# A fused conditioning and mixture-of-experts kernel: first silu and a gate product moved up, eight comparisons on GpSimd, one weight load and three second matrices moved in SyncE's queue

## The reference

```python
w = weights[conditions]                      # [32, 32, 32], itok picks the rows
xt = einsum('bct,bcd->bdt', x, w)            # x is 32 x 32 x 256: T = 1024 tokens, D = 256
probs = softmax(xt @ w_router)               # 16 experts
top_w, top_i = top_k(probs, 4); top_w /= sum(top_w)
g = silu(xt @ we1[e]) * (xt @ we3[e])        # H = 128, for each chosen expert
moe = sum over the chosen of top_w * (g @ we2[e])
shared = silu(xt @ ws1) * (xt @ ws3) @ ws2   # HS = 512, four units of 128
out = x + shared / 5 + moe * 4 / 5
```

## Time and profile before

| | |
|---|---|
| median of three runs | 146.99 us (146.42 to 147.77) |
| profiled execution | 146.96 us, span 145.2 us |
| TensorE busy | 132.4 us, 91% of the span |
| VectorE, ScalarE, GpSimd busy | 102.8, 71.6 and 65.6 us |
| granted TensorE clock | 1.0 of full speed |
| DMA | 29.82 MB, mean 205 GB/s |

### The profile page before, as it was taken

One profiled execution on the slowest core, in us unless ns is written; L12 is line 12 of the kernel. 1 busy time (PEld: TensorE's weight loads), 2 busy tenths in 40 slices (PEclk: granted clock), 3 DMA queues, 4 the chain that ended last, 5 costly groups with the idle time before them and its releaser, 6 DMA issues.

```text
span 145.2 us, 2783 instructions
## 1 busy us (share of the span) xinstructions
PE 132.4 (91%) x800; PEld 111.2 (77%) x800; DVE 102.8 (71%) x271; ACT 71.6 (49%) x164; POOL 65.6 (45%) x79
## 2 busy tenths in 40 slices
PE   5997998599989599999999999999999999999680
PEld 2437677388758488999999999999999978888560
DVE  1301799997769977877898989876677653157992
ACT  4003797999547454346353645377434331008900
POOL 0600000002777877656666776767576777100000
PEclk9999999999999999999999999999999999999999
DMA  1823799988955667687677755544542222399924
GB/s 36 294 59 84 218 287 272 379 247 257 365 204 167 188 188 207 163 251 227 184 249 232 254 212 220 187 165 169 186 178 86 97 108 103 74 387 423 385 79 144
DMA packets 23742, 29.82 MB, mean 205 GB/s; under 512 B 4112, under 2 KB 20496, under 8 KB 23600
## 3 DMA queue, kind: packets, MB, share of 16 engines
q1 hardware_dynamic: 19632, 19.86, 41.3%
q0 software_dynamic: 3120, 8.52, 18.0%
q10 hardware_dynamic: 976, 1.26, 2.4%
HBM read 17.58 MB, written 6.42 MB: 165 GB/s over the span
## 4 chain that ended last, share of the span: by engine, by line
PE 64%; DMA 12%; DVE 9%; ACT 6%; POOL 3%; issue 3%; ACTq 1%; DVEq 0%; SPq 0%; POOLq 0%
PE up_ps L1021 19%; PE down_ps L1037 14%; PE gate_ps L974 7%; PE up_ps L918 4%; PE gate_ps L918 4%; PE up_ps L1015 4%; PE down_ps L999 4%; PE down_ps L931 4%; POOL store_t L451 3%; DMA xt<-store_t 3%; DMA itok_rows<-in_itok_B 2%; DMA store_t<-y_of,token_i 2%; DMA g<-in_L_cond_weights,cond_idx 2%; ACT w_hi L482 2%; DVE raw L809 2%
## 5 line engine op out<-in xcount | busy, mean ns | idle before, releaser
L451 POOL DMA_INDIRECT store_t<-y_of,token_i x32 | 31.3, 979 | 41.1 <-DVE token_i L720 27.8
L458 POOL DMA_INDIRECT result<-store_t,back_i x32 | 31.4, 980 | 12.9 <-DVE store_t L802 7.1
L802 DVE SCALAR_TENSOR_TENSOR store_t<-down_ps,valid,store_t 128x256 f32 x47 | 21.5, 458 | 8.4 <-DVE store_t L802 4.9
L1037 PE MATMUL down_ps<-w,gt 128*128 x94 | 24.4, 381 | 0.0
L1021 PE MATMUL up_ps<-w_hi,x_hi 128*128 x78 | 23.6, 303 | 0.0
L1021 PE MATMUL up_ps<-w_hi,x_lo 128*128 x78 | 22.0, 282 | 0.0
L1021 PE MATMUL up_ps<-w_lo,x_hi 128*128 x78 | 22.0, 282 | 0.0
L559 ACT ACTIVATE gt<-down_ps 128x256 f32<-128x256 f32 (+1 forms) x24 | 9.1, 380 | 21.3 <-PE down_ps L999 21.2
L1037 PEld LDWEIGHTS down_ps<-w,gt 128*128 128x128 f32 x94 | 16.3, 190 | 1.9 <-issue 0.5
L567 ACT ACTIVATE sil<-up_ps 128x256 f32<-128x256 f32 (+1 forms) x24 | 9.1, 379 | 15.3 <-PE up_ps L1021 11.2
L974 PE MATMUL gate_ps<-ident,xt 128*128 128x128 f32 x94 | 14.3, 274 | 2.2 <-DMA xt<-store_t 1.6
(11 more groups left out here) (158 smaller groups left out, 240.9 us busy)
## 6 DMA issues: line engine op xcount, KB each, us to landing
xt<-store_t SPq DMA_DIRECT2D x43, 128.0 KB
raw<-in_L_ffn_we SPq DMA_DIRECT2D x30, 128.0 KB, 3.3
w<-in_L_ffn_we SPq DMA_DIRECT2D x4, 512.0 KB, 6.7
w_lo<-result SPq DMA_DIRECT2D x4, 512.0 KB, 6.7
raw<-result SPq DMA_DIRECT2D x4, 512.0 KB, 6.5
acc<-in_x SPq DMA_DIRECT2D x2, 512.0 KB, 4.5
y_of<-store_t ACTq DMA_DIRECT2D x1, 1024.0 KB, 6.0
out<-acc SPq DMA_DIRECT2D x3, 256.0 KB, 2.2
```

The costliest lines, as they stand in the source:

```text
L451: pool.indirect_dma_start(xs[:, j, :], None, y_of, bass.IndirectOffsetOnAxis(ap=token_i[:, j:j + 1], axis=0),).then_inc(tile_in[j % TT], 16)
L458: pool.indirect_dma_start(result, bass.IndirectOffsetOnAxis(ap=back_i[:, j:j + 1], axis=0), merged[:, j, :], None,).then_inc(result_out[j ...
L802: dve.scalar_tensor_tensor(out=into, in0=out_ps[n % 2][:, h, :], scalar=valid[:, it:it + 1], in1=into, op0=ALU.mult, op1=ALU.add).then_inc ...
L1037: last = pe.matmul(out_ps[b][:, h, :], gt[:, b, h, :], w2_of(experts[2 + h]), start=True, stop=True)
```

## The change

Five edits, all of order or place; the arithmetic is the same.

1. ScalarE does `shared_silu(0)` before the fourth copy of `y_row`, not after the store of `y_of` and three `high` copies.
2. TensorE does `gate_up(2, 0)` before `down(0)`. It waits for three of the four `y_row` copies before `gate_up(1, 0)` and for the fourth before `down(0)`. `down(2)` is no longer parted by `item_rows()`.
3. The last eight of the 32 comparisons that make `row_hot` move from VectorE to GpSimd, behind a wait for `row_f`, and TensorE waits for them by a semaphore of their own.
4. VectorE does `item_rows()` before `gated(2)`.
5. SyncE issues `load(0)` right behind the store of `cond_of`, ahead of the wait for its landing. The second matrices of experts 13 to 15 are loaded behind the copies of pair 5; those of experts 0 to 12 stay where they were, as three DMAs. TensorE waits for the late ones at pair 4.

```diff
+    SECOND_BEHIND = 5
@@ SyncE
             sp.dma_start(cond_of.rearrange("b (a n) -> (b a) n", a=4), cond_g).then_inc(cond_kept, 16)
+            load(0)
             sp.wait_ge(cond_kept, 16)
...
             sp.wait_ge(cond_in, 16 * Q)
-            load(0)
             load(1)
...
-            for q in range(4):
-                e = slice(q * E // 4, (q + 1) * E // 4)
-                sp.dma_start(w_2[:, e, :], we2[e].rearrange("e h d -> h e d")).then_inc(w_2_in, 16)
+            def load_second(e):
+                return sp.dma_start(w_2[:, e, :], we2[e].rearrange("e h d -> h e d"))
+
+            for e in (slice(0, 4), slice(4, 8), slice(8, E - LATE)):
+                load_second(e).then_inc(w_2_in, 16)
...
                     load(LOAD_BEHIND[n])
+                if n == SECOND_BEHIND:
+                    load_second(slice(E - LATE, E)).then_inc(w_2_last, 16)
@@ GpSimd
+            pool.wait_ge(row_f_done, 1)
+            for n in range(TK - TT, TK):
+                pool.tensor_scalar(row_hot[:, n, :], count_r[:, :], row_f[:, n:n + 1], None, ALU.is_equal).then_inc(last_hot_done, 1)
             pool.wait_ge(y_kept, 16)
@@ ScalarE
             for j in range(4):
+                if j == 3:
+                    shared_silu(0)
...
             for s in range(STEPS):
-                shared_silu(s)
+                if s:
+                    shared_silu(s)
@@ VectorE
-            chain(dve.tensor_copy(row_f[:, :], row_i[:, :]))
+            dve.tensor_copy(row_f[:, :], row_i[:, :]).then_inc(row_f_done, 1)
+            dve.wait_ge(row_f_done, 1)
...
-            for c in range(1, TOP_K):
+            for c in range(1, TOP_K - 1):
                 rows_hot(c)
             gated(1)
...
             item_bounds()
+            item_rows()
             gated(2)
-            item_rows()
@@ TensorE
                     if n % TT == 0:
-                        pe.wait_ge(row_hot_done, n + TT)
+                        if n < TK - TT:
+                            pe.wait_ge(row_hot_done, n + TT)
+                        else:
+                            pe.wait_ge(last_hot_done, TT)
...
             gate_up(0, 1)
-            pe.wait_ge(row_out, 4)
+            pe.wait_ge(row_out, 3)
             gate_up(1, 0)
             gate_up(1, 1)
-            pe.wait_ge(w_2_in, 16)
-            down(0)
             pe.wait_ge(dve_lo, 2)
             gate_up(2, 0)
+            pe.wait_ge(w_2_first, 16)
+            pe.wait_ge(row_out, 4)
+            down(0)
             choices()
...
-            down(2, [0])
             item_rows()
-            down(2, [1])
+            down(2)
...
-            pe.wait_ge(w_2_in, 16 * 5)
+            pe.wait_ge(w_2_in, 16 * 3)
...
+                    if 2 * n == LATE_ITEM[UNITS - LATE]:
+                        pe.wait_ge(w_2_last, 16)
```

More of the change, by code:

```diff
@@ L237, in adaln_ffn @@
         dest_hot_done = sem("dest_hot_done")
+        row_f_done = sem("row_f_done")
         row_hot_done = sem("row_hot_done")
+        last_hot_done = sem("last_hot_done")
         inverted = sem("inverted")
@@ L245, in adaln_ffn @@
         w_in = [sem(f"w_in{n}") for n in range(E + NSH)]
+        w_2_first = sem("w_2_first")
         w_2_in = sem("w_2_in")
+        w_2_last = sem("w_2_last")
         w_2_late = sem("w_2_late")
@@ L362, in _ @@
             sp.wait_ge(cond_in, 16 * Q)
-            load(0)
             load(1)
-            sp.dma_start(w_2[:, E:E + FRONT, :], ws2[0:FRONT * H].rearrange("(s h) d -> h s d", h=H)).then_inc(w_2_in, 16)
+            sp.dma_start(w_2[:, E:E + FRONT, :], ws2[0:FRONT * H].rearrange("(s h) d -> h s d", h=H)).then_inc(w_2_first, 16)
             load(UNITS - LATE)
@@ L500, in _, with shared_silu @@
             high(1)
+            def shared_silu(s):
+                h = s % 2
+                act.wait_ge(gate_done, s + 1)
+                if s >= 2:
+                    act.wait_ge(g_done, s - 1)
+                if s == 1:
+                    act.wait_ge(slot_done, 1)
+                act.activation(sil[:, h, :], gate_ps[h][:, :], ACT.Silu).then_inc(silu_done, 1)
             for j in range(4):
+                if j == 3:
+                    shared_silu(0)
                 if j == 1:
```

## The result

| | before | after |
|---|---|---|
| median | 146.7 us (4 runs, 145.77 to 147.77) | 148.96 us (4 runs, 147.03 to 150.05) |
| ratio to before | | 1.012 (1.006 to 1.018) |
| profiled execution | 146.96 us, span 145.2 | 147.03 us, span 145.3 |

The same kernel was timed in two more groups, twelve executions each: 147.29 us, ratio 1.002 (0.998 to 1.007), and 147.43 us, ratio 1.001 (0.998 to 1.004), where the medians before were 146.94 both times. The ratios leave out every execution more than 1.5% above the fastest of its kernel, so they can differ from the quotient of two medians. So the change is not the gain of 1.1 us that was forecast. It is a loss of 0.3 to 0.5 us in two groups, hardly to be told from none, and of 2.3 us in the small first one.

What follows compares the result with a forecast made beforehand. It took the time to be set by when pair 2 can be turned (49.10 us) and TensorE's work behind it. Terms 0.7 - 0.2 + 0.6 = 1.1 us took 146.96 to 145.9 us; range 144.9 to 147.2.

Steps and rivals of the forecast that it cites:

- I take 0.2 us, nearer to the lower end: Blocks queued behind load(0): their landing is delayed by 0.2 us, a loss on the chain of everything.
- ScalarE's 0.7 us: Table load and silu moved into ScalarE's idle time: the first gather comes 0.7 us earlier.
- most of 256 KB has moved before the blocks' packets are there: SyncE's queue at load(0): the reason given for a block delay near the lower end, 0.2 us.
- The bound of 1.3 us: Upper end for the blocks' delay: they wait for all of load(0)'s data, 1.3 us.
- I take 0.3 us: GpSimd's eight moved comparisons: 0.3 us each, after a 128x128 bfloat16 select at 0.29 us.
- my slack of 0.66: GpSimd's comparisons ahead of choices(): up to 0.66 us each costs nothing.
- the first rival: VectorE's and GpSimd's comparisons exclude each other: token_i only 0.15 us earlier, 146.4 us; chance 0.15.
- Behind them on GpSimd stands only the wait for the gathers: GpSimd's queue after the eight comparisons: nothing else there to delay, so no further cost was counted.
- I take 0.6 us: Pair 2's copy and pair 3's second gather land sooner: gain 0.6 us, between ends 0 and 1.1.
- The rest follows: Rounds behind pairs 2 and 3: everything later also comes 1.1 us earlier.
- 2.0 with no loss at the blocks: Rival of landings that come fully: gain 1.6, or 2.0 us, time 145.3 down to 144.9; chance 0.27.
- The slower rival: GpSimd's comparison as dear as a gather's issue, 1.08 us: 149.0 us, decisive from 0.85 each; chance 0.05.

Runs made afterwards that it cites:

- b1: Kernel before with only load(0) moved behind the store of cond_of: 147.94 us, ratio 1.006.
- a0: The whole changed kernel, run again as the base of its group: 147.29 us, ratio 1.002.
- c4: The whole changed kernel, run once more as the base of a later group: 147.43 us, ratio 1.001.
- b2: Changed kernel with both DMA moves undone, leaving the engines' order and the comparisons on GpSimd: 146.97 us, ratio 1.002.
- a1: Changed kernel with load(0) back behind the blocks: 146.42 us, ratio 0.999.
- the filled run: Changed kernel, DMA moves undone, loads of units 16 and 17 one pair earlier, eight added transposes before pairs 2 and 3 each: 146.82 us.
- e1: Kernel before with eight tiny memsets added on GpSimd ahead of the gathers: 146.85 us, ratio 1.001.
- c3_vector_unit16: Changed kernel with load(0) back, loads of units 16 and 17 one pair earlier, all comparisons on VectorE: 146.15 us, ratio 0.993.
- d3_order_vector: Changed kernel with both DMA moves undone, loads of units 16 and 17 one pair earlier, all comparisons on VectorE: 146.27 us, ratio 0.994.
- b3_load_back_unit16: Changed kernel with load(0) back behind the blocks and loads of units 16 and 17 one pair earlier: 146.01 us, ratio 0.995.
- d1_second_unit16: Kernel before with the late second matrices and loads of units 16 and 17 one pair earlier: 146.14 us, ratio 0.996.
- a2: Changed kernel with all 32 comparisons back on VectorE: 146.76 us, ratio 0.997.
- e2: Changed kernel with all comparisons on VectorE and eight tiny memsets on GpSimd in their place: 146.90 us, ratio 1.001.

## Why the prediction was wrong

**The blocks behind load(0).** This is the step that failed first: "I take 0.2 us, nearer to the lower end". It was 0.78 us in the first profile, 0.5 to 0.6 in the six others with the move, and b1 alone costs 0.6% of the time. In the first profile it ate the whole of ScalarE's 0.7 us: `token_i` ended at 34.39 after 34.38; in a0 and c4 0.2 to 0.3 us were left. SyncE had issued both loads in time, as I had it (7.88 to 9.12), and the landing was late all the same. "From the four loads' rate the data moves for about 1.3 us" took the pace at which SyncE issues for the pace of the data, which moved from about 9.2 to past 10.5 us; "most of 256 KB has moved before the blocks' packets are there" was half. The bound of 1.3 us held.

**ScalarE's order.** Right, in place and size. Without the moved load `token_i` is 0.58 us earlier (b2), with the blocks 0.2 us late there, and 0.76 us earlier (a1) with the blocks in time.

**GpSimd's comparisons.** "I take 0.3 us" was wrong: 0.66. That still fell within my slack of 0.66, and `choices()` waited for nothing that showed. VectorE's 24 took 0.37 us longer in all (1.55 + 2.88 against 1.39 + 2.67), nothing like the 1.7 us of the first rival, so that rule's result did not come. What I had wrong is the sentence "Behind them on GpSimd stands only the wait for the gathers": the eighth gather, the one that pair 3 waits for, is then issued 0.45 us later behind the first than before. I had named pair 3 as the bound and costed the edit at nothing beyond `token_i`.

**The landings.** "I take 0.6 us" was a hope, and the term is not there at pair 3. Pair 2 did come early (46.95). So it did in every other profile but the one with added work (by 48.4), those of before's own order included (47.4 to 48.4): 49.10 was mostly that one profile's bad luck, and little of the 2.15 us was gained by the change. The first four gathers did land 2.9 us after their issue, where it was 4.0 to 5.9 before, but those are not pair 3's. T3 lies between 49.6 and 51.9 us over the profiles (the filled run aside), 51.3 in the profile of before and 51.4 in that of after. I read one execution's worst landing as a reserve for the change, though the kernel before has the same chance of a better one: its executions spread from 145.65 to 149.11. A term of that kind belongs in the range, not in the sum.

**Behind pair 3.** "The rest follows" is the second failed step. I looked for new waits at pairs 4 and 6. The bound was unit 16's load, which the prediction does not name: with its place as before and pair 3 at 50.1 to 50.9, round 9 took 3.5 to 4.6 us in five of six such profiles, e1 in the order of before among them. Its split stands in ScalarE's and VectorE's queues. Moving the second matrices behind pair 5 puts one more load ahead of it. In the first profile of after this did not show, since pair 3 was not early (round 9 2.95 us); there the tail took the 0.5 us that the rounds had gained.

**The size.** The terms of the sum, by the runs: ScalarE's order -0.6 to -0.8, as predicted; blocks +0.5 to +0.8 and not +0.2; landings nothing and not -0.6; and, not in the sum, the eighth gather +0.45 behind the first. In the three profiles of the change the eighth gather was issued 0.2 to 0.5 us later than before, and the one early pair 3 (a0) was given back in round 9. That fits the 0.3 to 0.5 us by which the two medians of twelve are higher, but no run shows that it adds up so, and the intervals of both ratios include 1. One sum of the prediction is off: the rival's gain "2.0 with no loss at the blocks" is 0.7 + 1.1 = 1.8, so the range began 0.2 us too low; nothing hangs on it. The first group's 148.96 stays partly open. Two of its four executions had a mean clock of 0.987 and 0.981, and c4 shows what that costs; the one of 148.73 had a clock of 1.0, and nothing here explains it. The slower rival that I had priced, a comparison of 0.85 us or more, was not it, though its 149.0 us is that group's median: the comparisons took 0.66 us.

## What to carry to other kernels

A load that is issued in time to be out of the way need not be out of the way: small transfers right behind it came 0.5 to 0.8 us late here, on the chain of everything. When a stage is to start earlier, list every transfer whose time is fixed by something else (here a load in a queue behind copies that wait for gathers) and where its consumers stand in the queues of other engines: a gain passes only to the first of them. And of a landing time read once, take the middle of many, not the hope that the bad one goes away.

The four versions that beat the kernel before beyond their interval all have unit 16's load one pair earlier: c3_vector_unit16 at 146.15 us, 0.7% under before (0.3 to 1.0%), d3_order_vector at 146.27, 0.6% (0.3 to 1.0%), b3_load_back_unit16 at 146.01, 0.5% (0.2 to 0.8%), and d1_second_unit16 at 146.14, 0.4% (0.1 to 0.7%). They are not told from each other.

## What the hardware showed that I had not expected

GpSimd's first gathers behind its own comparisons are slower: the fifth takes 1.24 us against 0.95, and from the first to the eighth it is 9.42 us against 8.81, in nine profiles against four of the same order (a2, c3, d3, e2). A part of that is that the slow gathers stand one place earlier. A comparison of 128x128 bfloat16 takes 0.66 us there and 0.17 on VectorE. TensorE's clock fell to half behind a wait of 1.9 us for pair 3 in one profile, and did not behind waits of 2.1 and 2.4 us in two others.
